# First attention, first aggregation layer: the closing addition S + T on GpSimd in place of VectorE, with row maxima of one tile moved ahead of the diagonal update

## The chip, the cores and the metric

One Trainium2 chip, one core. The metric is the device time of one execution in microseconds, the median of several. The whole program is four layers (attention and feed-forward each) in one launch; only the first attention is touched.

## The reference

The input `x` has 2 batches of 1024 tokens with 128 features. The first attention, with 16 heads of width 64, computes (shortened):

```python
q, k, v = heads(xn @ Wq) * scale, heads(xn @ Wk), heads(xn @ Wv)
attn = softmax(where(causal_mask, mask_value, q @ k.T))
out = attn @ v
adj = clip(attn + eye(n), 0.0, 1.0)
deg = sum(adj, axis=-1)
feats = v
for l in range(2):
    h = feats @ gnn_w[l] + gnn_b[l]
    h = (adj @ h) / deg
    feats = gelu(h + feats)
out = out + feats @ lin_w + lin_b
return layer_norm(out @ Wo, gamma_out)
```

All is float32. The feed-forward layers and the three later attentions follow with a residual each; they are the same before and after.

## The kernel before

The stage works through 16 units: one pair of heads of one batch each, eight per batch. `for_units` runs `first`, then for each batch a body, a loop of six bodies and a last body, then a tail and the output projection with its layer norm. Every engine has its own copy of that walk, its instructions in one fixed order written out by hand; semaphores with running counts tie them together. A unit's body overlaps two units: the scores, exponentials and first aggregation of unit g, and then the projections, row maxima and first scores of unit u = g + 1 between the pieces of unit g's second aggregation.

Tiles: `E` holds exp(scores) of both heads, transposed, as the blocks on and above the diagonal (8 x 8 tiles of 128 x 128, for each head). `S`, `T`, `F1`, `F1B`, `VB`, `VW` are 128 partitions x 1024 and are handled in two halves c = 0 and c = 1 of 512 columns.

The first aggregation layer of unit g, step by step:

- TensorE sums E over keys, and `turn_sums` (L687) brings the sums to token rows. VectorE's `sums` (L902 to L913) makes from them small vectors `small`: 1/deg and the weight of the diagonal. `small_ready` releases what follows.
- TensorE's `product1` (L695, by L698) multiplies the aggregate by the layer's weight into the PSUM bank `prod`. VectorE's `scaled` (L917) multiplies it by 1/deg into `S`, half by half, and counts `s1a_done`.
- GpSimd forms `T` for each half: `VW` times a part of `small` (L389), plus `VB` (L392), which is the value plus bias. It counts `t1_done`.
- VectorE's `out1` (L937) adds S and T, half by half, and counts `s1_done`. ScalarE's `gelu1` (L447) waits for it and writes `F1`. ScalarE's order has `keep_v` of the next unit's half 1 behind `gelu1` of half 0.
- VectorE's `set_own` (L931) adds the diagonal weight to each of the 16 diagonal tiles of `E` in place, one instruction each, and counts `own_set`.
- TensorE then makes the second aggregation (`aggregate(F1, ...)`, L643). Before the step of key tile jt in half 0 it waits for `own_set` of 2 jt + 2, and before all of it for `gelu1` of half 0. Before the steps of half 1 from jt = 4 on it waits for gelu1 of half 1 and all 16. Between the steps of half 1 stand `row_scores` (L576, with the mask L580) of the next unit's tiles 3 to 7; tiles 0, 1, 2 stand ahead of the aggregation.
- VectorE's `row_max` (L867, and L871 with L873 for tiles 4 to 7) reduces each such score tile, from two PSUM buffers `ring` that alternate: the scores of tile 2 need tile 0's maxima, tile 3 needs tile 1's, tile 4 needs those of tiles 2 and 3. For tiles 4 to 7 `widen_high` (L879) spreads the maxima over SBUF columns.
- `max_rows` (L610) turns the maxima, and `score(u, 0)` and `score(u, 1)` (L628) open the next unit.
- GpSimd, after T, waits for all 16 `own_set`, then makes the quotient of the previous unit (L356), its output (L365), `F1B` (L400), the next unit's `VB` (L350) and, when VectorE has scaled the second layer, `out2` (L371).

`mix` (L731) is the last product of the previous unit; it waits for `s1a_done` of half 1 because it overwrites `prod`.

VectorE's order in the body, where the change is:

```python
scaled(S, g, 0, p1_ready, s1a_done)
out1(g, 0)
if more:
    row_max(u, 0)
scaled(S, g, 1, p1_ready, s1a_done)
out1(g, 1)
set_own(g)
if more:
    row_max(u, 1, 2, 3, 4, 5)
out2(g, 0)
```

`more` is false in the very last unit, which has no next one.

Of the kernel before, what the change touches and what calls it, by code (L numbers as in the profile page):

```python
# [5 lines left out]
ALU = mybir.AluOpType  # L6
# [170 lines left out]
def l0_attention(nc, d, x, xnT, ident, norm):  # L177

    with ExitStack() as ctx:
# [34 lines left out]
        T = sb("T", [P, ST * 2, DH])  # L214
        F1 = sb("F1", [P, ST, P])
        F1B = sb("F1B", [P, ST, P])
        S = sb("S", [P, ST * 2, DH])
# [34 lines left out]
        p1_ready, s1a_done, s1_done = sem("p1_ready"), sem("s1a_done"), sem("s1_done")  # L252
        t1a_done, t1_done, gelu1_done, f1b_done = sem("t1a_done"), sem("t1_done"), sem("gelu1_done"), sem("f1b_done")
# [36 lines left out]
        def heads8(t, c):  # L290

            return t[:, 8 * c:8 * c + 8, :]
# [23 lines left out]
        @block.sync  # L316
        def _(sp):
            def load(rows):
                sp.dma_start(wp[:, 0:3 * P], d["wqkv"][rows, :]).then_inc(w_in, 16)
                sp.dma_start(wvT[:, :], d["wvT"][rows, :]).then_inc(w_in, 16)  # L320

            def weights(rows, u):
                sp.wait_ge(vw_ready, u * 2)
                load(rows)

            for b in range(NB):
                with sp.Fori(0, PAIRS - 1) as i:
                    g = i + b * PAIRS if b else i
                    weights(bass.ds((i + 1) * P, P), g + 1)
                if b < NB - 1:  # L330
                    weights(slice(0, P), PAIRS * (b + 1))

        @block.gpsimd
        def _(pool):

            pool.memset(one[:, :], 1.0).then_inc(pool_step, 1)
            pool.memset(cap[:, :], 3.0e38).then_inc(pool_step, 1)
            pool.wait_ge(pool_step, 2)
            pool.affine_select(out=cap[:, :], in_=cap[:, :], compare_op=ALU.is_ge, fill=-1.0e38, base=0,
                               pattern=[[1, P]], channel_multiplier=-1).then_inc(pool_step, 1)  # L340
            pool.wait_ge(const_in, NCONST)

            def add_bias(src, row):
                return src, gnnb[row][:, :].unsqueeze(1).broadcast_to([P, 4, P])

            def keep_vb(u):
                for c in range(2):
                    pool.wait_ge(v_kept, u * 2 + (c + 1))
                    t = slice(4 * c, 4 * c + 4)
                    pool.tensor_tensor(VB[:, t, :], *add_bias(VH[:, t, :], 0), ALU.add).then_inc(vb_done, 1)  # L350

            def quotient(n, at):
                for c in range(2):
                    pool.wait_ge(inv_done, n * ST - (4 - 4 * c))
                    pool.wait_ge(ua_kept, n * 2 - (1 - c))
                    pool.tensor_tensor(half(AT, c), half(AT, c), half(UA, c), ALU.mult).then_inc(at_done, 1)  # L356
                flat = OT[:, :, :].rearrange("p a b -> p (a b)")
                for c in range(2):
                    pool.wait_ge(at_done, n * 2 - (1 - c))
                    pool.wait_ge(gl_kept, n * 2 - (1 - c))  # L360
                    if isinstance(at, int):
                        dst = OT[:, at - 1, c * 512:(c + 1) * 512]
                    else:
                        dst = flat[:, bass.ds(at * SEQ + (c * 512 - SEQ), 512)]
                    pool.tensor_tensor(dst, half(AT, c), gl(c), ALU.add).then_inc(ot_kept, 1)  # L365

            def out2(g, c):
                pool.wait_ge(s2a_done, g * 2 + (c + 1))
                pool.wait_ge(f1b_done, g * 2 + (c + 1))
                s = heads8(S2, c).rearrange("p a w -> p (a w)")  # L370
                pool.tensor_tensor(s, s, tiles4(F1B, c), ALU.add).then_inc(s2_done, 1)  # L371

            def body(g, prev, nb):
                wait(pool, s_ready, g)
                for jt in range(1, ST):
                    pool.wait_ge(exp_done, g * NP + through[jt])
                    w = SEQ - P * jt
                    dst = acc[:, :, SEQ - P - w:SEQ - P]
                    if jt == 1:
                        src = E[:, :, P:SEQ]  # L380
                    else:
                        src = dst
                        pool.wait_ge(acc_done, g * 7 + (jt - 1))
                    pool.tensor_tensor(dst, src, E[:, :, ecol[jt]:ecol[jt] + w], ALU.add).then_inc(acc_done, 1)  # L384
                pool.wait_ge(small_ready, g + 1)
                pool.wait_ge(vw_kept, g * 2 + 2)
                pool.wait_ge(vb_done, g * 2 + 2)
                for c in range(2):
                    pool.tensor_tensor(heads8(T, c), VW[:, 4 * c:4 * c + 4, :].rearrange("p a (h w) -> p (a h) w", w=DH),  # L389
                                       spread(small[:, 3, 8 * c:8 * c + 8], [P, 8, DH]), ALU.mult).then_inc(t1a_done, 1)  # L390
                    pool.wait_ge(t1a_done, g * 2 + (c + 1))
                    pool.tensor_tensor(heads8(T, c), heads8(T, c), VB[:, 4 * c:4 * c + 4, :].rearrange("p a (h w) -> p (a h) w", w=DH),  # L392
                                       ALU.add).then_inc(t1_done, 1)
                pool.wait_ge(own_set, g * 16 + 16)
                if prev is not None:
                    quotient(g, prev)
                for c in range(2):
                    pool.wait_ge(gelu1_done, g * 2 + (c + 1))
                    t = slice(4 * c, 4 * c + 4)
                    pool.tensor_tensor(F1B[:, t, :], *add_bias(F1[:, t, :], 1), ALU.add).then_inc(f1b_done, 1)  # L400
                if nb is not None:
                    pool.wait_ge(t1_done, g * 2 + 2)
                    keep_vb(g + 1)
                out2(g, 0)
                out2(g, 1)

            for_units(pool, lambda: keep_vb(0), body, quotient, lambda b: None)

        @block.scalar
# [434 lines left out]
        def _(dve):  # L844
# [17 lines left out]
            def row_max(u, *tiles):  # L862
                for it in tiles:
                    w = (it + 1) * P
                    if it < 4:
                        dve.wait_ge(rowmax_ready, u * NMAX + (it + 1))
                        dve.tensor_reduce(mx[:, :, it], pair(it % 2)[:, :, 0:w], AX_X, ALU.max).then_inc(max_done, 1)  # L867
                    else:
                        n = 4 + 2 * (it - 4)
                        dve.wait_ge(rowmax_ready, u * NMAX + (n + 1))  # L870
                        dve.tensor_reduce(mx[:, :, it], pair(0)[:, :, :], AX_X, ALU.max).then_inc(max_done, 1)  # L871
                        dve.wait_ge(rowmax_ready, u * NMAX + (n + 2))
                        dve.tensor_reduce(mxb[:, :, it - 4], pair(1)[:, :, 0:w - 512], AX_X, ALU.max).then_inc(max_done, 1)  # L873
                        widen_high(u, it)
# [56 lines left out]
                        dve.scalar_tensor_tensor(e_tile(h, jt, jt), ident[:, :], small[:, 2, k:k + 1], e_tile(h, jt, jt),  # L931
                                                 ALU.mult, ALU.add).then_inc(own_set, 1)

            def out1(g, c):
                dve.wait_ge(s1a_done, g * 2 + (c + 1))
                dve.wait_ge(t1_done, g * 2 + (c + 1))
                dve.tensor_tensor(heads8(S, c), heads8(S, c), heads8(T, c), ALU.add).then_inc(s1_done, 1)  # L937

            def out2(g, c):
                if c == 0:  # L940
                    wait(dve, s2_done, g * 2)
# [2 lines left out]
            def body(g, prev, nb):  # L944
                if prev is not None:
                    inverse(g, 0, 1)
                for jt in range(1, ST):
                    own_score(g, jt)
                    if prev is not None:
                        inverse(g, *{1: (2, 3), 2: (4, 5), 3: (6, 7)}.get(jt, ()))  # L950
                u = g + 1
                more = nb is not None
                if more:
                    keep_q_lo(u)
                    keep_k_lo(u)
                sums(g)
                dve.wait_ge(small_ready, u)
                scaled(S, g, 0, p1_ready, s1a_done)
                out1(g, 0)
                if more:  # L960
                    row_max(u, 0)
                scaled(S, g, 1, p1_ready, s1a_done)
                out1(g, 1)
                set_own(g)
                if more:
                    row_max(u, 1, 2, 3, 4, 5)
                out2(g, 0)
                if more:
                    row_max(u, 6, 7)
                    own_score(u, 0)  # L970
                out2(g, 1)
# [2057 lines left out]
```

## Time and profile before

| | |
|---|---|
| median of 3 runs | 1985.84 us (1979.84 to 1988.86) |
| the profiled execution | 1981.71 us, span 1979.9 us |
| TensorE matmul busy | 1519.4 us, 77% of the span |
| VectorE busy | 1292.6 us, 65% |
| GpSimd busy | 866.3 us, 44% |
| ScalarE busy | 753.3 us, 38% |
| mean granted TensorE clock | 0.870 |

Busy time is the time an engine executes; the rest is waiting or issuing. The first attention fills about the first half of the span, to some 1003 us. In the profile's rows a line number (L931) is a line of the kernel, an arrow `out<-in` names tiles, and `x16` after a shape is a count of instructions. In a timeline the columns are the start in us from the span's start, the duration in us of the merged row, engine, line, operation, tiles, shapes and, in brackets, the idle time ahead of it and the instruction whose end ended that idle time. Neighbouring instructions of an engine may overlap by a few hundredths.

### The profile page before, as it was taken

The page shows a single profiled execution, that of the slowest core. Times are in us where ns is not written, and L with a number is a line of the kernel's source. Part 1 is how long each engine was busy: PE and PEld are TensorE (multiplying, and loading weights), DVE is VectorE, ACT ScalarE, POOL GpSimd, SP SyncE. Part 2 cuts the span into 40 slices and gives each one's busy share as a digit, 9 for nine tenths or more (in the row PEclk, how much of TensorE's full clock was granted, in tenths as well). Part 3 has the DMA queues.
Part 4 walks back from the last instruction along what each step waited for, and adds up shares of the span by engine and source line. Part 5 has one row for each costly group of instructions (what it writes and reads, how often), then busy time and mean ns, then how long its engine had stood idle before and what let it go on. Part 6 is the DMA issues. An engine that isn't in the chain of part 4 may idle for free. (4 is left out here: it accounts for less than half of the span.)

```text
span 1979.9 us, 25385 instructions
## 1 busy us (share of the span) xinstructions
PE 1519.4 (77%) x8217; PEld 892.6 (45%) x8217; DVE 1292.6 (65%) x2913; ACT 753.3 (38%) x1153; POOL 866.3 (44%) x568
## 2 busy tenths in 40 slices
PE   3999999999899999999846779753229447677547
PEld 2554555555655555555623556533217212222447
DVE  5477777777667767777386544676503789989514
ACT  1444454454344545444335222321012364445112
POOL 0456655665446656565510100001143138898234
PEclk9899999999999999999779767875569768978758
DMA  1000000000000000000000000004120222211242
GB/s 53 6 1 6 5 5 5 5 5 6 1 6 6 5 5 5 0 5 0 1 13 0 7 6 10 20 0 181 26 62 21 59 68 81 84 66 53 33 139 74
DMA packets 47646, 56.36 MB, mean 28 GB/s; under 512 B 8769, under 2 KB 35034, under 8 KB 47314
## 3 DMA queue, kind: packets, MB, share of 16 engines
q1 hardware_dynamic: 44658, 49.40, 8.2%
q0 software_dynamic: 2912, 6.02, 0.9%
q8 instruction: 39, 0.64, 0.1%
q14 instruction: 37, 0.30, 0.0%
HBM read 42.85 MB, written 12.15 MB: 28 GB/s over the span
## 5 line engine op out<-in xcount | busy, mean ns | idle before, releaser
L486 ACT ACTIVATE l0a_E<-l0a_ring 128x1024 f32<-128x1024 f32 x192 | 150.4, 810 | 186.0 <-DVE l0a_scrap L892 178.9
L384 POOL TENSOR_TENSOR l0a_acc<-l0a_acc,l0a_E 128x1536 f32<-128x1536 f32 (+2 forms) x96 | 201.0, 2094 | 9.1
L2651 PE MATMUL mx_ysum<-mx_hst,main_ident 128*128 128x512 f32 x256 | 143.6, 697 | 41.2 <-POOL mx_hst L2770 34.2
L2785 POOL TENSOR_TENSOR mx_dBu<-mx_XI,mx_BB 128x1024 f32<-128x1024 f32 x64 | 139.5, 2207 | 47.8 <-DVE mx_DT L2825 47.8
L643 PE MATMUL l0a_agg<-l0a_E,l0a_VH 128*64 128x512 f32 (+3 forms) x768 | 150.8, 499 | 0.1
L643 PE MATMUL l0a_agg<-l0a_E,l0a_F 128*64 128x512 f32 (+3 forms) x768 | 149.1, 505 | 0.0
L887 DVE TENSOR_TENSOR l0a_ring<-l0a_ring,l0a_cap 128x256 f32<-128x256 f32 x128 | 55.0, 430 | 108.8 <-PE l0a_ring L633 108.8
L2754 ACT ACTIVATE mx_dA<-mx_DT,mx_A 128x512 f32<-128x512 f32 x128 | 87.7, 690 | 93.7 <-DVE mx_hst L2874 93.6
L925 DVE RECIPROCAL l0a_AT<-l0a_RB 128x128 f32<-128x128 f32 x128 | 111.9, 920 | 1.5
L2651 PEld LDWEIGHTS mx_ysum<-mx_hst,main_ident 128*128 128x128 f32 x256 | 54.8, 222 | 114.8 <-issue 56.1
L384 POOL TENSOR_TENSOR l0a_acc<-l0a_E 128x1792 f32<-128x1792 f32 x16 | 64.4, 4027 | 81.0 <-ACT l0a_E L486 81.0
L628 PE MATMUL l0a_ring<-l0a_QH,l0a_KH 64*128 64x512 f32 (+3 forms) x384 | 81.4, 420 | 19.1 <-ACT l0a_E L486 17.3
L165 PE MATMUL n_turned<-main_ident,n_xn 128*128 128x128 f32 x96 | 25.8, 455 | 90.5 <-DVE n_xn L135 90.5
L576 PE MATMUL l0a_ring<-l0a_KH,l0a_QH 64*128 64x512 f32 (+3 forms) x384 | 80.2, 438 | 19.4 <-DVE l0a_mx L871 5.5
L2874 DVE TENSOR_TENSOR_SCAN mx_hst<-mx_dA,mx_hst,mx_dBu 128x512 f32<-128x512 f32 x64 | 82.1, 1282 | 7.2
L628 PEld LDWEIGHTS l0a_ring<-l0a_QH,l0a_KH 64*128 64x128 f32 x384 | 36.5, 187 | 109.7 <-ACT l0a_E L486 67.3
L371 POOL TENSOR_TENSOR l0a_S<-l0a_S,l0a_F1B 128x512 f32<-128x512 f32 x32 | 40.9, 1277 | 100.7 <-DVE l0a_S L917 100.7
L389 POOL TENSOR_TENSOR l0a_T<-l0a_VW,l0a_small 128x512 f32<-128x512 f32 x32 | 33.4, 1044 | 112.3 <-DVE l0a_small L913 112.3
L871 DVE TENSOR_REDUCE l0a_mx<-l0a_ring 128x2 fp32r<-128x1024 f32 x64 | 78.1, 1220 | 5.0 <-PE l0a_ring L576 5.0
L576 PEld LDWEIGHTS l0a_ring<-l0a_KH,l0a_QH 64*128 64x128 f32 x384 | 35.2, 186 | 101.6 <-DVE l0a_mx L871 32.4
L892 DVE SCALAR_TENSOR_TENSOR l0a_scrap<-l0a_ring,main_ident 128x128 f32<-128x128 f32 x256 | 74.5, 291 | 8.9
L2874 DVE TENSOR_TENSOR_SCAN mx_hst<-mx_dA,mx_dBu 128x512 f32<-128x512 f32 x64 | 77.4, 1209 | 0.0
(487 smaller groups left out, 3730.6 us busy)
## 6 DMA issues: line engine op xcount, KB each, us to landing
mx_BB<-mx_brows SPq DMA_DIRECT2D x32, 512.0 KB, 3.6
me_W<-in_f_w SPq DMA_DIRECT2D x16, 256.0 KB, 9.5
l0a_wp<-in_wqkv SPq DMA_DIRECT2D x16, 192.0 KB, 2.3
moe_Wg<-in_f_wg SPq DMA_DIRECT2D x8, 256.0 KB
moe_Wu<-in_f_wu SPq DMA_DIRECT2D x8, 256.0 KB
moe_Wd<-in_f_wd SPq DMA_DIRECT2D x8, 256.0 KB
moe_Y<-rt_zeros SPq DMA_DIRECT2D x2, 1024.0 KB, 10.8
e_back<-moe_Y SPq DMA_DIRECT2D x8, 256.0 KB, 4.6
```

The costliest lines, as they stand in the source:

```text
L384: pool.tensor_tensor(dst, src, E[:, :, ecol[jt]:ecol[jt] + w], ALU.add).then_inc(acc_done, 1)
L486: act.activation(E[:, :, at:at + n], pair(k % 2)[:, :, 0:n], ACT.Exp).then_inc(exp_done, 1)
L576: mm = pe.matmul(pair(r)[:, h, 0:c1 - c0], QH[hi(h), it * P:(it + 1) * P], KH[hi(h), c0:c1], start=True, stop=c1 <= it * P)
L628: pe.matmul(out[:, h, 0:n], a[hi(h), keys], b[hi(h), at], start=a is KH and b is QH, stop=False, skip_group_check=True)
L643: mm = pe.matmul(agg[c][cols, lo - 512 * c:512], feats[:, jt, cols], E[:, h, at + lo:at + hi], start=(jt == 0), stop=(jt == 4 * c + 3), sk ...
L871: dve.tensor_reduce(mx[:, :, it], pair(0)[:, :, :], AX_X, ALU.max).then_inc(max_done, 1)
L892: dve.scalar_tensor_tensor(scrap[:, :], pair(k % 2)[:, h, 0:P], 1.0, ident[:, :], ALU.mult, ALU.mult, accum_out=eii[:, jt, h:h + 1]).then_ ...
L925: dve.reciprocal(AT[:, t], RB[:, t]).then_inc(inv_done, 1)
L2651: mm = pe.matmul(ysum[h][:, c * 512:(c + 1) * 512], ident[:, :], hst[:, k % DEEP, c * 512:(c + 1) * 512], start=(n == 0), stop=(n == NS - ...
L2754: act.activation(dA[:, c * 512:(c + 1) * 512], DT[:, h, b * SEQ + c * 512:b * SEQ + (c + 1) * 512], ACT.Exp, scale=A[:, h, n:n + 1]).then_ ...
L2785: pool.tensor_tensor(dBu[:, k % DEEP, :], du_of(h, b), BB[:, q % 3, :], ALU.mult).then_inc(dBu_ready, 1)
L2874: dve.tensor_tensor_scan(hst[:, k % DEEP, half], dA[:, half], dBu[:, k % DEEP, half], hst[:, k % DEEP, 511:512] if c else 0.0, ALU.mult, A ...
```

## The change

GpSimd makes the addition S + T of each half right after it has completed T, once VectorE has scaled S. VectorE loses both additions. It takes the row maxima of tile 1 before `set_own`, and waits there for both halves of S.

```diff
@@ gpsimd, body
                     pool.tensor_tensor(heads8(T, c), heads8(T, c), VB[...], ALU.add).then_inc(t1_done, 1)
+                    pool.wait_ge(t1_done, g * 2 + (c + 1))
+                    pool.wait_ge(s1a_done, g * 2 + (c + 1))
+                    pool.tensor_tensor(heads8(S, c), heads8(S, c), heads8(T, c), ALU.add).then_inc(s1_done, 1)
                 pool.wait_ge(own_set, g * 16 + 16)
@@ vector
-            def out1(g, c):
-                dve.wait_ge(s1a_done, g * 2 + (c + 1))
-                dve.wait_ge(t1_done, g * 2 + (c + 1))
-                dve.tensor_tensor(heads8(S, c), heads8(S, c), heads8(T, c), ALU.add).then_inc(s1_done, 1)
@@ vector, body
                 scaled(S, g, 0, p1_ready, s1a_done)
-                out1(g, 0)
                 if more:
                     row_max(u, 0)
                 scaled(S, g, 1, p1_ready, s1a_done)
-                out1(g, 1)
+                if more:
+                    row_max(u, 1)
+                dve.wait_ge(s1_done, g * 2 + 2)
                 set_own(g)
                 if more:
-                    row_max(u, 1, 2, 3, 4, 5)
+                    row_max(u, 2, 3, 4, 5)
                 out2(g, 0)
```

## Rows read from the trace of the kernel before

**Rows 1.** Table of stretches, one steady unit: bounds, length, busy us per engine, clock.
```profile
370.50:426.50 56.00, 54.05 (x340) 29.61 (x339) 40.72 (x94) 27.17 (x42) 34.04 (x22) 1.00 0.02 5
```

**Rows 2.** Table of waits, TensorE, 45 to 990 us: us in total, times, longest.
```profile
PE l0a_prod L731 <- DVE l0a_S L917: 6.3, 14, 0.9
PE l0a_ring L576 <- DVE l0a_mx L871: 5.5, 15, 0.8
```

**Rows 3.** Timeline of GpSimd in one steady unit.
```profile
426.13 1.04 POOL L389 TENSOR_TENSOR l0a_T<-l0a_VW,l0a_small 128x512 f32<-128x512 f32 x1 [6.97 <-DVE l0a_small L913]
427.25 1.27 POOL L392 TENSOR_TENSOR l0a_T<-l0a_T,l0a_VB 128x512 f32<-128x512 f32 x1
428.47 1.05 POOL L389 TENSOR_TENSOR l0a_T<-l0a_VW,l0a_small 128x512 f32<-128x512 f32 x1
429.60 1.60 POOL L392 TENSOR_TENSOR l0a_T<-l0a_T,l0a_VB 128x512 f32<-128x512 f32 x1
436.44 2.51 POOL L356 TENSOR_TENSOR l0a_AT<-l0a_AT,l0a_UA 128x512 f32<-128x512 f32 x2 [5.24 <-DVE l0a_E L931]
```

**Rows 4.** Timeline of VectorE in the same unit.
```profile
428.62 1.45 DVE L937 TENSOR_TENSOR l0a_S<-l0a_S,l0a_T 128x512 f32<-128x512 f32 x1 [1.91 <-POOL l0a_T L392]
...
431.30 0.69 DVE L937 TENSOR_TENSOR l0a_S<-l0a_S,l0a_T 128x512 f32<-128x512 f32 x1 [0.30 <-POOL l0a_T L392]
431.91 4.28 DVE L931 SCALAR_TENSOR_TENSOR l0a_E<-main_ident,l0a_small,l0a_E 128x128 f32<-128x128 f32 x16
436.11 1.55 DVE L867 TENSOR_REDUCE l0a_mx<-l0a_ring 128x2 fp32r<-128x512 f32 x2
```

**Rows 5.** Timeline of TensorE in the same unit.
```profile
432.11 0.39 PE L576 MATMUL l0a_ring<-l0a_KH,l0a_QH 64*128 64x256 f32 x2
...
433.24 2.38 PE L643 MATMUL l0a_agg<-l0a_E,l0a_F 128*64 128x512 f32 x16
...
442.21 0.62 PE L576 MATMUL l0a_ring<-l0a_KH,l0a_QH 64*128 64x512 f32 x4
...
447.07 0.50 PE L576 MATMUL l0a_ring<-l0a_KH,l0a_QH 64*128 64x512 f32 x2 [0.31 <-DVE l0a_mx L871]
447.93 0.51 PE L576 MATMUL l0a_ring<-l0a_KH,l0a_QH 64*128 64x512 f32 x2 [0.36 <-DVE l0a_mxb L873]
...
450.03 0.50 PE L628 MATMUL l0a_ring<-l0a_QH,l0a_KH 64*128 64x512 f32 x2
```

**Rows 6.** Timeline, same unit: VectorE's widenings and a maximum, then GpSimd's later operations.
```profile
441.40 1.38 DVE L879 TENSOR_TENSOR l0a_mw<-l0a_mx,l0a_mxb 128x128 fp32r<-128x128 f32 x1
...
444.62 0.66 DVE L879 TENSOR_TENSOR l0a_mw<-l0a_mx,l0a_mxb 128x128 fp32r<-128x128 f32 x1
...
447.91 0.29 DVE L879 TENSOR_TENSOR l0a_mw<-l0a_mx,l0a_mxb 128x128 fp32r<-128x128 f32 x1
448.12 1.22 DVE L871 TENSOR_REDUCE l0a_mx<-l0a_ring 128x2 fp32r<-128x1024 f32 x1
...
441.35 2.56 POOL L400 TENSOR_TENSOR l0a_F1B<-l0a_F,l0a_gnnb 128x512 f32<-128x512 f32 x2
443.87 2.55 POOL L350 TENSOR_TENSOR l0a_VB<-l0a_VH,l0a_gnnb 128x512 f32<-128x512 f32 x2
446.38 1.27 POOL L371 TENSOR_TENSOR l0a_S<-l0a_S,l0a_F1B 128x512 f32<-128x512 f32 x1
```

**Rows 7.** Timeline, first unit of the second batch: VectorE and TensorE.
```profile
568.26 4.28 DVE L931 SCALAR_TENSOR_TENSOR l0a_E<-main_ident,l0a_small,l0a_E 128x128 f32<-128x128 f32 x16
...
569.24 3.23 PE L643 MATMUL l0a_agg<-l0a_E,l0a_F 128*64 128x512 f32 x20
...
573.20 0.50 PE L576 MATMUL l0a_ring<-l0a_KH,l0a_QH 64*128 64x512 f32 x2 [0.73 <-DVE l0a_mx L867]
```

**Rows 8.** Timeline, the last unit: GpSimd and TensorE.
```profile
955.71 1.04 POOL L389 TENSOR_TENSOR l0a_T<-l0a_VW,l0a_small 128x512 f32<-128x512 f32 x1 [9.02 <-DVE l0a_small L913]
...
962.31 4.24 PE L643 MATMUL l0a_agg<-l0a_E,l0a_F 128*64 128x512 f32 x16
```

## The prediction

> **What bounds the kernel now.** The edit sits in the first attention, so I read that stage by units (one pair of heads of one batch, 16 in all). The table of stretches comes first: in one steady unit of 56.00 us TensorE is busy 54.05, VectorE 40.72, GpSimd 34.04, at granted clock 1.00, the upper of the two levels (2.4 GHz) [rows 1]. TensorE is the bound; only 1.95 us of a unit are its idle time, and its instruction stream is in order, so a new stall in it lengthens the unit unless a later stall shrinks. The table of TensorE's own waits names the candidates for shrinking: the wait of L731 for the scaled tile (6.3 us in all, 0.43 a unit) and the wait of L576 for the later row maxima (5.5, some 0.36 a unit) [rows 2]. The other idle time lies in pieces too small for that table to group.
>
> Then the timelines of one steady unit, engine by engine, around the edited step. GpSimd forms T in four operations: 1.04, 1.27, 1.04 and 1.60 us from 426.13 on, and next works at 436.44, after the sixteenth own_set [rows 3]. VectorE adds T to S at 428.62 and 431.30, starts set_own at 431.91 (16 instructions, 4.28 us) and takes the maxima of row tiles 1 and 2 at 436.11 [rows 4]. TensorE starts the second aggregation at 433.24 without any idle time ahead of it [rows 5]. Its first matmuls need two of the set_own results. At 4.28/16 = 0.27 us apart these are complete at about 431.91 + 0.27 + 0.35 (the one that reads 0.35 us long is the last to end) = 432.5, so VectorE is now 0.7 us ahead of TensorE there.
>
> **The change, part by part.**
>
> *Removed from VectorE:* two additions a unit, 1.45 and 0.69 us [rows 4], 2.14 us. The first stands there at 1.45 because it ran beside a GpSimd operation until 429.52. They are worth something only where VectorE is the last to arrive.
>
> *Added to GpSimd:* the same two additions, in its one queue, between the first tile's T and the second tile's T, and after the latter. No addition of this form by GpSimd precedes set_own, but L392 is of the same size, type and number of SBUF inputs: 1.27 alone and 1.60 when it began beside VectorE's addition [rows 3]. That one is gone, so I take 1.27 for all four additions. The bounds of such an addition are 0.69 (what VectorE needs) and 1.60. A dependent start costs 0.08 (427.25 after 427.17). The chain: multiply 1.04, +0.08 add 1.27, +0.08 new add 1.27 gives s1 of tile 0 at 429.87, against 430.07 before; then multiply 1.04 (it follows at once, 0.05 overlapped), +0.08 add 1.27, +0.08 new add 1.27: s1 of tile 1 at 433.57, against 431.99 before.
>
> The Trainium skill speaks against this side of the move. GPSIMD Engine Reference, 4.1 Engine selection, keeps elementwise additions on VectorE and calls GpSimd about 2 times slower for two inputs. The uncontended rows here, 1.27 against 0.69, are 1.84 times; a factor of 2 would put the new additions at 1.38 and add 0.2 us to each unit.
>
> *The new wait on VectorE.* set_own now waits for s1 of tile 1. Behind it in VectorE's queue stand set_own itself, the remaining row maxima, the second scaling and the next unit's diagonal work; TensorE's second aggregation waits for set_own, and GpSimd's quotient, F1B, VB and S2 additions wait for its sixteenth result. A GpSimd result reached VectorE 0.10 us later (428.52 to 428.62), so set_own starts at 433.67, 1.76 later than now. The first pair is complete at 434.28, TensorE sees it at about 434.35, and it stands ready since 433.24: a **new stall of 1.1 us**. The pace afterwards is no problem: a pair of set_own takes 0.54, a step of TensorE with 512 columns more.
>
> *The row maxima of tile 1, moved ahead of set_own.* TensorE delivers that tile's scores at 432.11 plus 0.6, the reduction of 512 elements takes about 0.7 (tiles 1 and 2 together, 512 and 768 elements, take 1.55 [rows 4]) and ends at 433.4, just under the 433.57 that VectorE would wait for anyway: it costs nothing, covered by GpSimd's last addition; without that cover it would push set_own by 0.7. What it brings: TensorE's scores of tile 3 no longer wait for set_own plus tile 1. In a steady unit they did not; in the two first units of a batch they did, 0.73 us [rows 7]. The wait of L731 (0.43) is fed by the scaling of tile 1, which needs product1 and cannot start noticeably earlier; whatever it gave would be swallowed by the stall behind it.
>
> *What comes back, and what it collides with.* From the first widening on VectorE works at maxima without a pause, and TensorE waits for it at 447.07 (0.31) and 447.93 (0.36) [rows 5]. Row by row the widening of L879 shows an effect: 1.38 us when started at 441.40, with GpSimd's F1B pair running from 441.35; 0.66 at 444.62 beside the VB pair; 0.29 at 447.91, when GpSimd had stopped at 447.65 [rows 6]. Each ends some 0.2 us after a GpSimd operation ends: VectorE was held until then. The maxima themselves (from PSUM) are not held. Now GpSimd's sequence moves by 1.76 and VectorE's by 1.1. Widening 1 starts at 442.5 and is let in at 443.35 (now 442.78: shift 0.6). The maximum of tile 5 needs TensorE's scores of 442.21 [rows 5], their first half 0.3 later and all 1.1 later: it starts at 443.65 instead of 442.76. Widening 2, 0.9 later at 445.5, is held to the end of F1B, now 1.76 later at 445.67, and ends at 445.85 (now 445.28). Widening 3 keeps its distance of 2.63 and starts at 448.5, but GpSimd's S2 addition now runs 448.15 to 449.4, so it ends at 449.6 where it ended at 448.15. The maximum of tile 7's first half (448.12, 1.22 us [rows 6]) ends at 450.8 instead of 449.34, and TensorE's next score at 450.03 [rows 5] becomes 450.85. **Net for a steady unit: +0.85 us**, between the stall with its full return (0) and stall plus full hold of widening 3 with none of widening 1's relief (1.1 + 0.3).
>
> The lock is the second place for the skill: SBUF — State Buffer, Who interferes with whom, says that a VectorE instruction with two SBUF inputs and a GpSimd instruction that reads SBUF exclude each other for the whole instruction, and that tensor_reduce never contends. The widening rows agree to 0.2 us. If bandwidth were merely shared instead, widening 3 would lose about half of its wait, and the unit would end at +0.6.
>
> *First unit of each batch (2).* Same chain from its own start: set_own at 568.26 + 1.76 = 570.02, first pair seen at 570.7, and TensorE, ready at 569.24, is 1.46 late [rows 7]. The wait of 0.73 goes, but tile 2's maximum, 0.87 of those 1.55 us, ends only at 575.1 (set_own's end 574.3 plus it), where it ended at 572.5 + 1.55 = 574.0, and the scores of tile 4 need it. **+1.1 each.**
>
> *Last unit (1).* No row maxima, a lower clock. GpSimd starts at 955.71; 7.43 + 0.10 + 0.62 + 0.07 later is 963.9, TensorE stood ready at 962.31 [rows 8]. **+1.6.** The layer norm and everything after start later by it and are otherwise the same.
>
> **Sum.** 13 x 0.85 + 2 x 1.1 + 1.6 = 14.9 us. On the profiled execution's 1981.71 us (span 1979.9 plus 1.8) that is 1996.6. The median of the runs, 1985.84, lies 4.1 above that execution; 15 us on it gives **2001 us**, 0.75% slower.
>
> **Rivals.**
> A. *Full absorption.* TensorE's new stall of 1.1 is paid back by the waits for maxima that follow (0.31 + 0.36, and the part of widening 1's hold that TensorE felt ahead of them), because widening 1 comes out of its hold and widening 3 does not enter one. Then steady units are +0 to +0.4 and the sum is 4 to 9 us: 1990 to 1995. For it: the waits of rows 2; against: widening 3's new neighbour. Chance 0.15.
> B. *Costlier additions.* L392 stays at 1.60 in the second tile, and the new additions too are held by something on VectorE: +0.3 to +0.7 a unit on the path to set_own, 20 to 26 us: 2006 to 2012. For it: the 1.60 in every unit; against: its partner on VectorE is removed. Chance 0.20.
> C. *The other side: faster.* VectorE is the bound from its first widening to its third; if its two holds all fell out because GpSimd's sequence moved (1.09 + 0.37 a unit), and TensorE's wait of 0.43 at L731 went with the freed 2.14 us, the unit would gain 1.9 against 1.1 lost, 0.8 x 13 - 3.8 = 6.6 us faster: 1979. It decides from the point where the relief exceeds the stall; GpSimd's operations run back to back for over 11 us there, so both falling out is hardly possible. Chance 0.04.
> D. *The wait is not binding:* set_own's results are not what TensorE reaches for first. Then nothing stalls, 1985 to 1988. The code gates the first matmul with two of them. Chance 0.03.
> Forecast as worked out: 0.58.
>
> **Numbers.** The range takes the forecast, most of A and most of B: 1990 to 2009. A measurement of this kernel tells about 0.5% (10 us) from no change. Slower by more: the forecast nearly all, B, hardly any of A: 0.76. Within: most of A, D and a part of the forecast: 0.20. Faster: 0.04.
>
> **What would show it.** On the changed trace of a steady unit: six GpSimd operations in a row, the last ending 7.4 us after the first began; a VectorE wait for GpSimd of about 0.2 us ahead of L931 (line numbers shift), a new TensorE wait of about 1.1 us for l0a_E at the second aggregation; GpSimd's next start at 438.2 in place of 436.44; first widening near 0.85, third near 1.1 in place of 0.29; unit length 56.85. It is wrong if the unit stays at 56.0, if TensorE shows no wait there, or if additions on GpSimd differ from 1.27.

## The result and the profile after

The changed kernel takes 2020.57 us (median of 4, 2017.17 to 2023.21) against 1987.35 us (median of 4, 1979.84 to 1990.47): ratio 1.0169, 95% interval 1.0145 to 1.0193. It is 33 us slower where 15 were forecast, outside the range. Before, the profiled execution took 1981.71 us, after, 2023.21 us (span 2021.4).

The change did what it says. Two rows of the page give VectorE's and GpSimd's busy time: VectorE fell by 27.5 us, GpSimd rose by 34.8 us.

```profile
PE 1528.5 (76%) x8217; PEld 897.7 (44%) x8217; DVE 1265.1 (63%) x2881; ACT 756.3 (37%) x1153; POOL 901.1 (45%) x600
```

The stretch around the edited step follows, in the unit that answers to that of [rows 3 to 6]; it lies 12.47 us later (GpSimd's first T multiplication at 438.60, not 426.13). First GpSimd's timeline:

```profile
438.60 1.04 POOL L389 TENSOR_TENSOR l0a_T<-l0a_VW,l0a_small 128x512 f32<-128x512 f32 x1 [6.96 <-DVE l0a_small L916]
439.72 1.27 POOL L392 TENSOR_TENSOR l0a_T<-l0a_T,l0a_VB 128x512 f32<-128x512 f32 x1
441.07 1.27 POOL L396 TENSOR_TENSOR l0a_S<-l0a_S,l0a_T 128x512 f32<-128x512 f32 x1
442.30 1.04 POOL L389 TENSOR_TENSOR l0a_T<-l0a_VW,l0a_small 128x512 f32<-128x512 f32 x1
443.42 1.27 POOL L392 TENSOR_TENSOR l0a_T<-l0a_T,l0a_VB 128x512 f32<-128x512 f32 x1
444.77 1.27 POOL L396 TENSOR_TENSOR l0a_S<-l0a_S,l0a_T 128x512 f32<-128x512 f32 x1
450.60 2.50 POOL L356 TENSOR_TENSOR l0a_AT<-l0a_AT,l0a_UA 128x512 f32<-128x512 f32 x2 [4.57 <-DVE l0a_E L934]
...
455.51 2.55 POOL L403 TENSOR_TENSOR l0a_F1B<-l0a_F,l0a_gnnb 128x512 f32<-128x512 f32 x2
458.02 2.55 POOL L350 TENSOR_TENSOR l0a_VB<-l0a_VH,l0a_gnnb 128x512 f32<-128x512 f32 x2
460.54 1.26 POOL L371 TENSOR_TENSOR l0a_S<-l0a_S,l0a_F1B 128x512 f32<-128x512 f32 x1
```

The chain is as forecast: six operations, 7.44 us from first start to last end. The 1.60 of [rows 3] became 1.27. VectorE's timeline:

```profile
445.22 0.69 DVE L870 TENSOR_REDUCE l0a_mx<-l0a_ring 128x2 fp32r<-128x512 f32 x1 [1.81 <-PE l0a_ring L583]
446.07 4.29 DVE L934 SCALAR_TENSOR_TENSOR l0a_E<-main_ident,l0a_small,l0a_E 128x128 f32<-128x128 f32 x16 [0.16 <-POOL l0a_S L396]
...
454.90 0.80 DVE L882 TENSOR_TENSOR l0a_mw<-l0a_mx,l0a_mxb 128x128 fp32r<-128x128 f32 x1
456.26 1.23 DVE L874 TENSOR_REDUCE l0a_mx<-l0a_ring 128x2 fp32r<-128x1024 f32 x1 [0.55 <-PE l0a_ring L579]
...
458.11 1.33 DVE L882 TENSOR_TENSOR l0a_mw<-l0a_mx,l0a_mxb 128x128 fp32r<-128x128 f32 x1
...
462.08 0.29 DVE L882 TENSOR_TENSOR l0a_mw<-l0a_mx,l0a_mxb 128x128 fp32r<-128x128 f32 x1
```

set_own starts 0.03 us after GpSimd's last addition ended (446.04); VectorE had then been idle for 0.16, so the moved maximum was covered, by little. Of the three widenings (L879 in [rows 6]) the first fell from 1.38 to 0.80, the third stayed at 0.29, and the second, at 458.11, rose from 0.66 to 1.33: GpSimd's VB addition had begun at 458.02, 0.09 us earlier, and VectorE was held for all of its 1.27. TensorE's timeline shows both losses, as bracketed waits that [rows 5] have as none and 0.31:

```profile
446.74 2.38 PE L646 MATMUL l0a_agg<-l0a_E,l0a_F 128*64 128x512 f32 x16 [0.97 <-DVE l0a_E L934]
...
455.71 0.62 PE L579 MATMUL l0a_ring<-l0a_KH,l0a_QH 64*128 64x512 f32 x4
...
461.23 0.51 PE L579 MATMUL l0a_ring<-l0a_KH,l0a_QH 64*128 64x512 f32 x2 [0.97 <-DVE l0a_mx L874]
462.10 0.49 PE L579 MATMUL l0a_ring<-l0a_KH,l0a_QH 64*128 64x512 f32 x2 [0.36 <-DVE l0a_mxb L876]
...
464.19 0.50 PE L631 MATMUL l0a_ring<-l0a_QH,l0a_KH 64*128 64x512 f32 x2
```

From GpSimd's first multiplication to the aggregation it is 446.74 - 438.60 = 8.14 us; before it was 433.24 - 426.13 = 7.11: +1.03. From there to the next unit's first score it is 17.45 against 450.03 - 433.24 = 16.79: +0.66. Together 1.69 in this unit; the starts of L389 in neighbouring steady units are 57.65 apart in the median, where they were 56.00. The second part is the second widening's alone: it ends 458.11 + 1.33 - 446.74 = 12.70 after the start of the aggregation, where it ended 12.04 after it, and TensorE's wait at tile 7 grew by the same 0.66, from 0.31 to 0.97.

Two steady units, one in each batch, are longer still, 59.29 and 59.24 us. The table of stretches (after the columns of [rows 1]: the granted clock stands third from the end) shows one of them, right after its wait at tile 7:

```profile
343.00:344.00 1.00, 0.33 (x2) 0.00 (x0) 1.00 (x2) 0.00 (x0) 1.00 (x2) 1.00 0.00 0
344.00:345.00 1.00, 0.50 (x2) 0.19 (x2) 1.00 (x2) 0.00 (x0) 0.87 (x1) 1.00 0.00 0
345.00:346.00 1.00, 0.83 (x4) 0.34 (x4) 0.97 (x3) 0.00 (x0) 0.00 (x0) 0.65 0.00 0
346.00:347.00 1.00, 1.00 (x6) 0.46 (x6) 1.00 (x2) 0.00 (x0) 0.00 (x0) 0.50 0.00 0
347.00:348.00 1.00, 1.00 (x8) 0.41 (x6) 0.97 (x2) 0.00 (x0) 0.00 (x0) 0.50 0.00 0
348.00:349.00 1.00, 1.00 (x10) 0.55 (x8) 0.04 (x1) 0.05 (x1) 0.00 (x0) 0.65 0.00 0
349.00:350.00 1.00, 1.00 (x9) 0.55 (x9) 0.00 (x0) 0.55 (x1) 0.00 (x0) 1.00 0.00 0
```

TensorE was busy for 0.33 and 0.50 us of two stretches of 1 us, then the clock fell to 0.50, its lower level of 1.2 GHz, for some 3.3 us: the unit loses 1.6 us.

**Where the 33 us are.** Up to the end of the first attention the trace is 33.36 us behind that of before (the next layer's statistics start at 1037.35 against 1003.99). From the starts of L389: the 13 steady units 25.5 us, which is 13 x 1.67 = 21.7, twice 1.6 for the clock and 0.5 at the change of batch; the two first units 2.23 + 2.70 (each has a stretch at the lower clock that was not there); the last unit to the end of the stage 2.70; 0.27 before the first. The trace divides the first and last units further. These are the aggregations of the two first units and, with the product behind it, that of the last:

```profile
99.79 4.78 PE L646 MATMUL l0a_agg<-l0a_E,l0a_F 128*64 128x512 f32 x20 [1.06 <-ACT l0a_F L450]
...
587.08 5.18 PE L646 MATMUL l0a_agg<-l0a_E,l0a_F 128*64 128x512 f32 x20 [0.45 <-DVE l0a_E L934]
...
994.58 4.54 PE L646 MATMUL l0a_agg<-l0a_E,l0a_F 128*64 128x512 f32 x16 [3.27 <-ACT l0a_F L450]
999.05 1.91 PE L734 MATMUL l0a_prod<-l0a_FT,l0a_gnn_lin 128*128 128x512 f32 x2
```

In the first units they start 1.46 and 1.51 us late (counted from the unit's L389, as all starts here), the wait of 0.73 at tile 3 is gone, and at clock 0.50 they take 4.78 and 5.18 us where they took 3.23 [rows 7]: 1.46 - 0.73 + 1.55 = 2.28 and 1.51 - 0.73 + 1.95 = 2.73. In the last unit the aggregation starts 1.61 late and, with the lower clock lasting longer than before, takes 4.54 for 4.24 [rows 8] and the product 1.91 for 1.13: 2.69. In three units (both rows above with L450, and the last unit of the first batch) the profile puts the wait to ScalarE's second half of F1, which ends at about the same time as the first pair of set_own; the code asks here only for F1's first half, done over 3 us before, and for set_own.

The two medians differ by 33.2. The two profiled executions differ by a further 8 us in later stages, which the change doesn't touch and the medians don't show.

### The profile page after: what moved, and what is told of

It reads as the page before. It is cut to its first block and busy times, and to the rows that moved or that the text cites. A ratio compares the mean times of both kernels' runs of the same rounds, so it can differ in the third digit from the quotient of the medians.

```text
span 2021.4 us, 25385 instructions
## 1 busy us (share of the span) xinstructions
PE 1528.5 (76%) x8217; PEld 897.7 (44%) x8217; DVE 1265.1 (63%) x2881; ACT 756.3 (37%) x1153; POOL 901.1 (45%) x600
## 5 line engine op out<-in xcount | busy, mean ns | idle before, releaser
L2650 PE MATMUL mx_ysum<-mx_hst,main_ident 128*128 128x512 f32 x256 | 136.0, 664 | 51.4 <-POOL mx_hst L2769 43.1
L646 PE MATMUL l0a_agg<-l0a_E,l0a_F 128*64 128x512 f32 (+3 forms) x768 | 155.5, 524 | 17.4 <-DVE l0a_E L934 12.1
L870 DVE TENSOR_REDUCE l0a_mx<-l0a_ring 128x2 fp32r<-128x256 f32 (+1 forms) x64 | 52.6, 824 | 80.2 <-PE l0a_ring L583 80.2
L389 POOL TENSOR_TENSOR l0a_T<-l0a_VW,l0a_small 128x512 f32<-128x512 f32 x32 | 33.3, 1042 | 112.9 <-DVE l0a_small L916 112.9
L646 PEld LDWEIGHTS l0a_agg<-l0a_E,l0a_F 128*64 128x64 f32 x768 | 49.0, 143 | 71.6 <-issue 29.8
```

What stands on the lines that cost most here:

```text
L646: mm = pe.matmul(agg[c][cols, lo - 512 * c:512], feats[:, jt, cols], E[:, h, at + lo:at + hi], start=(jt == 0), stop=(jt == 4 * c + 3), sk ...
L2650: mm = pe.matmul(ysum[h][:, c * 512:(c + 1) * 512], ident[:, :], hst[:, k % DEEP, c * 512:(c + 1) * 512], start=(n == 0), stop=(n == NS - ...
```

## The experiments

Ten kernels; the ratio is to the kernel before on the same chip (e1 to e8 ran on one chip, e9 and e10 on another, and the median of the kernel before was 1991.72 us beside e1 to e4, 1986.06 beside e5 to e8 and 1986.78 beside e9 and e10). "Unit" is the distance of L389 in neighbouring steady units of the profile (there are 11 such distances within the batches); the wait at tile 7 is that ahead of its first half; the last column counts, of the 11, those with a stretch at the lower clock. Units, waits and counts are from one execution of each. Ratios of different kernels are compared only roughly: e3's units are those of the change, and its ratio is 0.35% lower.

| kernel | ratio (95%) | unit, us | wait at aggregation | wait at tile 7 | low clock, of 11 |
|---|---|---|---|---|---|
| before | 1 | 56.00 | none | 0.31 | 0 |
| the change | 1.0169 (1.0145 to 1.0193) | 57.65 | 0.97 | 0.97 | 2 |
| e1_free_own | 1.0115 (1.0088 to 1.0141) | 57.0 | none | 1.07 | 5 |
| e2_rowmax_only | 1.0138 (1.0112 to 1.0165) | 57.43 | 0.71 | 0.98 | 4 |
| e3_add_only | 1.0134 (1.0108 to 1.0160) | 57.67 | 0.97 | 0.97 | 2 |
| e4_after_spaced | 1.0082 (1.0051 to 1.0112) | 56.64 | 0.97 | none | 0 |
| e5_before_spaced | 0.9975 (0.9960 to 0.9991) | 55.60 | none | none | 0 |
| e6_spaced_late_out2 | 0.9964 (0.9946 to 0.9983) | 55.47 | none | none, 0.41 at the score | 0 |
| e7_dummy | 1.0137 (1.0110 to 1.0163) | 56.8 | none | 1.12 | 9 |
| e8_half | 1.0128 (1.0100 to 1.0155) | 57.00 | 0.28 | 0.98 | 4 |
| e9_best | 0.9933 (0.9911 to 0.9955) | 55.00 | none | none | 0 |
| e10_change_on_best | 1.0032 (1.0014 to 1.0049) | 56.05 | 0.97 | none | 0 |

### e1_free_own: set_own doesn't wait for GpSimd

```diff
-                if more:
-                    row_max(u, 1)
-                dve.wait_ge(s1_done, g * 2 + 2)
                 set_own(g)
                 if more:
-                    row_max(u, 2, 3, 4, 5)
+                    row_max(u, 1, 2, 3, 4, 5)
```

> The changed kernel, but VectorE starts set_own right after scaling tile 1 and takes the row maxima of tile 1 after it, as before; it no longer waits for GpSimd's additions. A steady unit was 56.00 us before and 57.65 with the change. Theory (the 1.03 us stall of TensorE is the wait of set_own for GpSimd's chain; a VectorE operation with two SBUF inputs is held while a GpSimd operation runs): set_own's operations get in only between GpSimd's operations of about 1.2 us, the first pair is ready near 432.5 on the old unit's time axis, TensorE's stall shrinks from 0.97 to 0.3 or less, and the unit is 56.2 to 57.0. Rival 1 (no hold; only the wait counts): set_own runs 4.3 us undisturbed beside GpSimd, no stall, unit 56.0 or slightly less. Rival 2 (the stall comes from elsewhere, for example from late F1 by way of ScalarE): unit stays at 57.6.

2013.01 us. The stall at the aggregation is gone (it starts 7.09 us after GpSimd's first multiplication, before 7.11), though F1 comes from GpSimd's additions here too; so the stall was set_own's wait for GpSimd and not late F1, and rival 2 falls. But the hold is there. In its timeline set_own starts at once and lasts 6.38 us in place of 4.28:

```profile
698.09 6.38 DVE L934 SCALAR_TENSOR_TENSOR l0a_E<-main_ident,l0a_small,l0a_E 128x128 f32<-128x128 f32 x16
...
712.14 1.42 DVE L882 TENSOR_TENSOR l0a_mw<-l0a_mx,l0a_mxb 128x128 fp32r<-128x128 f32 x1
```

Rival 1 falls with these 2.1 us. The unit is 57.0, at the upper end of what was expected: the second widening is held again (1.42), and TensorE waits 1.07 at tile 7.

### e2_rowmax_only and e3_add_only: each part alone

```diff
# e2, on the kernel before
                 out1(g, 1)
+                if more:
+                    row_max(u, 1)
                 set_own(g)
                 if more:
-                    row_max(u, 1, 2, 3, 4, 5)
+                    row_max(u, 2, 3, 4, 5)
# e3, on the changed kernel
-                if more:
-                    row_max(u, 1)
                 dve.wait_ge(s1_done, g * 2 + 2)
                 set_own(g)
                 if more:
-                    row_max(u, 2, 3, 4, 5)
+                    row_max(u, 1, 2, 3, 4, 5)
```

> The kernel before with one part of the change alone: the row maxima of tile 1 stand ahead of set_own; both additions stay on VectorE. Theory: VectorE now waits for TensorE's scores of tile 1 (432.75) and reduces to 433.4, so set_own starts 1.5 us later than before, TensorE stalls 0.9 at the second aggregation, GpSimd's sequence moves by 1.55 against TensorE's 0.9 and the second widening is held by the whole of a GpSimd addition as in the changed kernel: unit 57.4 to 57.6, total some 25 to 32 us over before. Rival (the slower additions on GpSimd are what costs; the moved reduction is free): unit 56.0, total within 5 us of before.

> The changed kernel with the other part alone: additions on GpSimd and the wait, but the row maxima of tile 1 after set_own as before. Theory: set_own starts when GpSimd's chain ends, as in the changed kernel, the later reduction fits into VectorE's 0.6 us of idle time ahead of tile 3; unit 57.6 to 57.8, total as the changed kernel within 4 us. Rival (the moved reduction is what costs): unit about 56.0 to 56.5.

2017.97 and 2018.20 us. The reduction moved by itself costs 1.43 us a unit, nearly as much as the whole change, and both expectations of the unit were met. In e2 VectorE waits for TensorE's scores, reduces, and only then starts set_own; both additions are still its own:

```profile
444.92 0.69 DVE L867 TENSOR_REDUCE l0a_mx<-l0a_ring 128x2 fp32r<-128x512 f32 x1 [0.76 <-PE l0a_ring L580]
445.52 4.28 DVE L931 SCALAR_TENSOR_TENSOR l0a_E<-main_ident,l0a_small,l0a_E 128x128 f32<-128x128 f32 x16
...
457.56 1.33 DVE L879 TENSOR_TENSOR l0a_mw<-l0a_mx,l0a_mxb 128x128 fp32r<-128x128 f32 x1
```

set_own starts 1.45 us later than before after the same point, 0.7 of which was margin, and the aggregation 0.78. The two parts' costs don't add, since both delay the same set_own: 1.43 and 1.67 us a unit alone, 1.65 together.

### e4_after_spaced: GpSimd keeps clear of the later widenings

```diff
                     pool.wait_ge(t1_done, g * 2 + 2)
+                    pool.wait_ge(mw_high, (g + 1) * 4 + 2)
                     keep_vb(g + 1)
+                    pool.wait_ge(mw_high, (g + 1) * 4 + 4)
                 out2(g, 0)
```

> The changed kernel, and GpSimd waits for the second widening before it makes VB and for the fourth before it makes the first S2 addition, so that neither runs when VectorE's later widenings start. Theory (0.64 us of each steady unit is the second widening held by GpSimd's VB addition, 1.33 against 0.29 us): second widening 0.3 us, TensorE's wait for the maxima of tile 6 back from 0.97 to 0.3 or less, unit 56.9 to 57.1 and the 1.6 us of half clock in units 4 and 11 gone or not, total 8 to 13 us under the changed kernel. Rival 1 (the hold is hidden behind TensorE; the unit's second loss has another cause): unit 57.65, total the same as the changed kernel. Rival 2 (GpSimd's sequence becomes too late for something): unit above 57.65.

2006.57 us, by the medians 14 under the changed kernel, by the ratios 17; 8 to 13 were expected. The second widening takes 0.29, TensorE's wait at tile 7 is gone, the stall of 0.97 at the aggregation remains, and no steady unit has a low clock:

```profile
440.45 2.38 PE L648 MATMUL l0a_agg<-l0a_E,l0a_F 128*64 128x512 f32 x16 [0.97 <-DVE l0a_E L936]
...
453.92 0.50 PE L581 MATMUL l0a_ring<-l0a_KH,l0a_QH 64*128 64x512 f32 x2
```

The unit fell by 1.01, more than expected (56.64 for 56.9 to 57.1): the whole hold of 1.33 - 0.29 = 1.04 us went, and 0.37 of it (0.66 for 0.29) the kernel before has too; the expectation had counted only the 0.64 that the change added. The first widening is held here as in the change (0.81). Making GpSimd wait twice made the changed kernel faster.

### e5_before_spaced and e6_spaced_late_out2: the same in the kernel before

```diff
# e5, on the kernel before: as e4, and ahead of F1B
+                if nb is not None:
+                    pool.wait_ge(mw_high, (g + 1) * 4 + 1)
# e6, on e5
-                    row_max(u, 1, 2, 3, 4, 5)
+                    row_max(u, 1, 2, 3, 4, 5, 6)
                 out2(g, 0)
                 if more:
-                    row_max(u, 6, 7)
+                    row_max(u, 7)
```

> The kernel before, with GpSimd waiting for the first widening before F1B, for the second before VB, and for the fourth before the first S2 addition. Theory (VectorE's widenings are held by GpSimd's additions, and TensorE feels it at tiles 6 and 7): widenings 0.3 us each in place of 1.38 and 0.66; VectorE's chain 0.5 us shorter by the third widening (the maximum of tile 5 then waits for TensorE); TensorE's waits at tile 7 shrink; unit 55.4 to 55.7 in place of 56.00, total 4 to 9 us under before. Rival (the holds are hidden, TensorE's own stream sets the pace there): unit 56.0, same time. Rival 2 (GpSimd late for something): slower.

> As e5_before_spaced, and VectorE scales the first half of the second layer (0.68 us) after the maxima of tile 6 in place of before them, so that TensorE gets tile 6's maxima earlier. Theory: TensorE's wait at tile 7 (0.31 and 0.36) all but goes, unit 55.0 to 55.4, total 8 to 13 us under before. Rival: the second half of tile 7 then waits for the delayed scaling and nothing is gained over e5_before_spaced.

1981.50 and 1982.81 us against 1986.06: both a little faster than before, not told apart from each other. e5 is as expected (unit 55.60, 4.6 us in all). e6 is not: its unit of 55.47 is above the 55.0 to 55.4 expected and its gain of 3 us (7 by the ratio) below the 8 to 13; its third widening met the VB addition (0.80 us) and passed 0.41 us on to TensorE's first score.

e5 also shows which hold counts. Its first widening takes 0.29 in place of 1.38, and the maximum of tile 5 behind it still starts 9.52 us after the aggregation, as before, now after a wait for TensorE's scores:

```profile
443.17 1.23 DVE L875 TENSOR_REDUCE l0a_mx<-l0a_ring 128x2 fp32r<-128x1024 f32 x1 [1.07 <-PE l0a_ring L580]
```

So the hold of 1.09 us at the first widening cost nothing, and the unit's gain of 0.40 is nearly all the 0.37 of the second.

### e7_dummy: the later wait without GpSimd

```diff
                                   ALU.max).then_inc(mw_high, 1)
+                if it == 5:
+                    dve.reciprocal(idle[:, :], ident[:, :])
```

> The kernel before with one useless reciprocal (128 columns, about 0.9 us, no SBUF input shared with GpSimd's work) on VectorE right after the second widening; nothing else. It puts the changed kernel's later wait of TensorE (tile 7) into the kernel before, without GpSimd. Theory (in that stretch TensorE follows VectorE one for one, and the half-clock stretches of about 3 us come after such a wait whatever causes it): TensorE's wait at tile 7 grows from 0.31 to 1.1 or 1.2, unit 56.8 to 56.9, and some steady units show a stretch at the lower clock and are 1.6 us longer still; total 11 to 20 us over before. Rival 1 (slack hides it): unit 56.0 to 56.3. Rival 2 (the clock falls only with both waits, at the aggregation and here): no steady unit at the lower clock.

2015.26 us. A useless 0.94 us on VectorE in an otherwise unchanged kernel costs 1.4% (1.0137), some 27 us: the unit grows by 0.8 (56.8 in the two steady units left undisturbed), and nine of the eleven are 58.2 to 58.4, with the clock at 0.50 after the wait:

```profile
462.54 0.50 PE L577 MATMUL l0a_ring<-l0a_KH,l0a_QH 64*128 64x512 f32 x2 [1.12 <-DVE l0a_mx L872]
463.40 0.79 PE L577 MATMUL l0a_ring<-l0a_KH,l0a_QH 64*128 64x512 f32 x2 [0.36 <-DVE l0a_mxb L874]
```

The second of these rows takes 0.79 where [rows 5] have 0.51. So the low clock needs neither the stall at the aggregation nor a change in GpSimd's work; rival 2 falls, and rival 1 too. It cost more than the 11 to 20 us expected, since the clock fell in nine units and not in "some".

### e8_half: one addition of the two

```diff
# on the changed kernel; GpSimd adds only for c == 0
-                if more:
-                    row_max(u, 1)
                 dve.wait_ge(s1_done, ...)
+                dve.tensor_tensor(heads8(S, 1), heads8(S, 1), heads8(T, 1), ALU.add).then_inc(s1_done, 1)
                 set_own(g)
```

> The changed kernel with only the addition of half 0 on GpSimd; half 1 is added by VectorE as before, and the maxima of tile 1 come after set_own as before. GpSimd's chain in front of set_own is one addition shorter. Theory (unit = 56.00 + stall at the aggregation + 0.65 for the second widening; once TensorE stalls at set_own at all, GpSimd and TensorE both start from set_own, so their distance and with it the hold of the widening are fixed): set_own starts 1.0 us later than before, stall 0.3 to 0.4, second widening 1.3 us, unit 56.9 to 57.1. Rival (the loss is in proportion to the moved work): unit 56.8. Rival 2 (the widening is held only at the changed kernel's larger shift): 56.3 to 56.4.

2009.64 us. The stall fell from 0.97 to 0.28, and the second widening is held as long as ever:

```profile
449.49 0.81 DVE L883 TENSOR_TENSOR l0a_mw<-l0a_mx,l0a_mxb 128x128 fp32r<-128x128 f32 x1
452.72 1.33 DVE L883 TENSOR_TENSOR l0a_mw<-l0a_mx,l0a_mxb 128x128 fp32r<-128x128 f32 x1
```

The aggregation starts 0.34 later than before after the same point, and the unit is 56.00 + 0.35 + 0.65 = 57.00 as the theory has it; rival 2 (56.3 to 56.4) falls, and the proportion of rival 1 would have been 56.8. Once TensorE stalls for set_own at all, it starts from set_own's first pair and GpSimd from its last one. Their distance no longer depends on how late set_own is: from aggregation to quotient 3.86 us in the change, in e2, in e3 and in e8, where it was 436.44 - 433.24 = 3.20. The second widening starts 11.38 after the aggregation in all of these and before; so it meets GpSimd's VB addition 0.66 us earlier in that addition's course, and is held 0.67 longer.

### e9_best and e10_change_on_best

```diff
# e9, on e6
-                    pool.wait_ge(mw_high, (g + 1) * 4 + 2)
+                    pool.wait_ge(mw_high, (g + 1) * 4 + 3)
                     keep_vb(g + 1)
```

e10 is the change made on e9.

> As e6_spaced_late_out2, and GpSimd's VB waits for the third widening in place of the second, since in e6_spaced_late_out2 the third widening was still held (0.80 us) by the first VB addition and TensorE waited 0.41 us for the maxima of tile 7 at the next unit's first score. Theory (each of TensorE's waits for maxima is a hold passed on): all widenings 0.29 us, that wait all but gone, steady unit 55.0 to 55.2 in place of 55.47, total 14 to 18 us under before. Rival (the wait of 0.41 is replaced by another, of the scores of the widened tiles or of TensorE for the scaled second layer): 55.3 to 55.5, total as e6_spaced_late_out2.

> The change made on top of e9_best, where no widening is held. Theory (with the holds out of the way the change costs its stall at set_own alone, 1.03 us a steady unit, and no stretch at the lower clock): unit 56.0 to 56.2, total 15 to 18 us over e9_best, near the kernel before. Rival (the freed 2.14 us of VectorE now pay, as VectorE is no longer held): 55.0 to 55.5, as e9_best. Rival 2 (the second cost was never the hold): 56.7 as e9_best plus 1.65.

1973.40 us, the fastest of all, 0.67% or 13 us under before and clear of it (14 to 18 were expected; the unit, 55.00, is as expected). Each later widening takes 0.29, and GpSimd's VB waits 3.15 us for them:

```profile
440.63 0.29 DVE L883 TENSOR_TENSOR l0a_mw<-l0a_mx,l0a_mxb 128x128 fp32r<-128x128 f32 x1
...
442.95 0.29 DVE L883 TENSOR_TENSOR l0a_mw<-l0a_mx,l0a_mxb 128x128 fp32r<-128x128 f32 x1
...
443.42 2.51 POOL L350 TENSOR_TENSOR l0a_VB<-l0a_VH,l0a_gnnb 128x512 f32<-128x512 f32 x2 [3.15 <-DVE l0a_mw L883]
```

On top of it the change costs 1.05 us a steady unit, its stall and nothing else: 1991.89 us, 18 over e9. In e10 the first widening is held again (0.80), as in the change, and the others are not (0.29 to 0.32), so the expectation's "no widening is held" was not quite met; the first one's hold costs nothing here either. The 2.14 us that the change takes from VectorE buy nothing. The move of VectorE's scaling behind the maxima of tile 6, without GpSimd's waits, was not run, so e9's gain is not divided between the two.

## Why the prediction was wrong

**Right: the direction and the first mechanism.** TensorE is the bound; set_own became the last to arrive. Chain 7.43 us forecast, 7.44 measured; stall 1.1 forecast, 1.03 longer to the aggregation (0.97 as a bracketed wait); all additions 1.27, so rival B's price for them didn't come, and the time, above even its 2006 to 2012, has other causes. e1 and e8 move the stall as the chain moves.

**Right that the move of the row maxima is covered, but only beside the additions.** The prediction said that without cover it would push set_own by 0.7. In e2 set_own starts 1.45 later, 0.76 of it a wait for TensorE's scores and 0.69 the reduction; after 0.7 of margin that leaves 0.78 at the aggregation, and with the held widening 1.43 a unit.

**Wrong: the step "what comes back, and what it collides with".** It forecast for widening 1 an end 0.6 late, a near miss for widening 2 and a full hold for widening 3, together 0.25 off the stall. Measured: widening 1 as forecast (0.80 for 0.85), widening 2 held whole (1.33), widening 3 free (0.29), together 0.66 on top of the stall. The failing term is the start of widening 2. On the forecast's time axis (the aggregation at 434.35) it was put at 445.5, 0.17 before the end of an F1B addition; measured, 11.37 after the aggregation, it is 445.7, just past that end and past the start of the VB addition. The error came in with the maximum of tile 5 ahead of it. That was shifted by 0.9, as if part of the first widening's relief passed through it; but TensorE's scores set its start, and they moved by the whole stall. The scores begin 8.97 after the aggregation in both kernels (442.21, 455.71), and the maximum starts 0.55 after that, not 0.3: 9.52 after the aggregation before and after (443.87 on the forecast's axis, 0.2 later than forecast). An error of 0.2 us in a start became one of 1.2 us in the end of widening 2 (447.05 for 445.85), because at the edge between two additions a hold is none or whole. Widening 3 then came later too, at 462.08, 0.28 after GpSimd's S2 addition had ended, and the hold forecast for it didn't come. Between its two ends for this step (0 and 1.4 a unit) the measured 1.67 wasn't, since the upper end had a hold of 0.3 for the third widening and none for the second.

**Missing: the clock.** No term stood for it. In the change it took 3.2 us in steady units, by the rows above 1.55 and 1.95 in the first units (2.23 and 2.70 measured for 1.1 each) and 1.1 in the last (2.7 for 1.6): some 7.8 us in all. All three aggregations started as late as forecast (1.46, 1.51, 1.61). That the change brings the low clock in the first units is not shown: e5, which touches nothing ahead of that aggregation, has it in its first unit too (57.15 us from L389 to L389, where before has 54.86).

**The exclusive hold.** It was borne out at each step: a widening of 0.29 us took 1.33 beside a 1.27 us addition in e8 and the change, set_own took 6.38 for 4.28 in e1, and 0.29 to 0.32 was left wherever the GpSimd addition of that moment was made to wait. The Trainium skill (SBUF — State Buffer, Who interferes with whom) says so of a VectorE operation with two SBUF inputs, and the trace agrees. Were bandwidth merely shared, the second widening would be about 0.6 (an estimate, twice 0.29).

**Rivals.** A (absorption) had the right place and the wrong sign: TensorE's waits at tile 7 didn't shrink but grew from 0.31 to 0.97. C and D fell with the trace. The sum: 13 x 1.67 + 3.2 + 0.5 + 4.9 + 2.7 + 0.3 = 33.3, for 14.9. Of the 18.4 between them, 10.7 are the steady units' 1.67 for 0.85 and some 7.8 the clock; the 0.5 and 0.3 are about made up by the first units, whose own delay was 1.46 - 0.73 and 1.51 - 0.73 where the forecast had 1.1 (it had tile 4's scores wait for tile 2's maximum, and in the trace they don't).

## What to carry to other kernels

Before work is given to an engine that is mostly idle, follow what it delays: here 0.7 us of margin at one gate was all that stood between a free engine and the bound. Where two engines exclude each other on some operations, list the start and end of each such pair after the shift; a collision foreseen as a near miss has to be priced as a full one. A relief counts only if the engine that gets it is the last to arrive at the next gate: 1.09 us less at the first widening bought nothing. An idle engine told to wait until the busy one's short operations are through can be worth more than the work moved to it: the waits alone gained 0.25% (e5), with one reordering on VectorE 0.67% (e9), where the moved additions cost 1.7%.

## What the runs showed of the hardware

A wait of TensorE costs more than itself when the clock falls behind it. In the kernels whose steady units have a wait of 0.97 to 1.12 us at tile 7, with 0.36 us more right after, two to nine of 11 units ran some 3.3 us at half clock behind it, 1.5 to 1.7 us each. In the kernels that have the wait of 0.97 us only at the aggregation (e4, e10) none of the 11 did. What besides the wait's place decides in which units it happens was not found, and the counts are of one execution each.
